# Vision tower on Trainium2: another order of loads and weight preparation at the start and at the end of the attention part

## The reference, cut to what matters

```python
# x: (32, 3, 256, 256)  ->  32 images; result (32, 257, 256)
gray  = einsum('bchw,c->bhw', x, (0.2989, 0.587, 0.114))
edges = conv3x3(gray, scharr, padding='SAME')          # two filters
edge  = abs(edges).sum(filters) / 2                    # 256 rows = 256 tokens of width 256
h = concatenate([cls_tok, edge])                       # 257 tokens
h = h + attention(layernorm(h))                        # 16 heads of 16, causal, w_qkv, w_out
h = h + ffn(layernorm(h))                              # w_gate, w_up (704x256), w_down (256x704)
# ffn: activations quantised with one scale from max|x| over ALL tokens of ALL images,
#      each weight row w: scale = max|w|/127, clip(round(w/scale))*scale
```

## Time and profile before

| | |
|---|---|
| median of 3 runs | 1169.92 us |
| the profiled execution, own time | 1166.12 us |
| its span | 1164.4 us |
| busy: PE, DVE, ACT, POOL | 949.2, 806.9, 686.8, 537.5 us |
| first scores (step 4) begin | 89.75 us |
| first instruction behind the barrier | 942.31 us |

### The profile page before, as it was taken

One profiled execution on the slowest core, in us unless ns is written; L12 is line 12 of the kernel. 1 busy time (PEld: TensorE's weight loads), 2 busy tenths in 40 slices (PEclk: granted clock), 3 DMA queues, 4 the chain that ended last, 5 costly groups with the idle time before them and its releaser, 6 DMA issues. The chain is left out here.

```text
span 1164.4 us, 28062 instructions
## 1 busy us (share of the span) xinstructions
PE 949.2 (82%) x9584; PEld 681.1 (58%) x9584; DVE 806.9 (69%) x1969; ACT 686.8 (59%) x1171; POOL 537.5 (46%) x685
## 2 busy tenths in 40 slices
PE   2268899989989999899999999989988458885665
PEld 1045666666766767676676766767666333332544
DVE  1735566777776677777767777776666359998687
ACT  0154666666666666666666666666554237785785
POOL 5243555566556555655656565556443242220000
PEclk9988999999999999999999999999998769998888
DMA  3854455555555556555455655554322005501874
GB/s 86 233 133 112 126 138 152 149 133 148 149 133 129 137 154 150 138 150 143 126 135 148 154 135 150 148 131 105 101 62 62 12 1 199 199 1 50 271 231 137
DMA packets 156101, 152.90 MB, mean 131 GB/s; under 512 B 28263, under 2 KB 152458, under 8 KB 153994
## 3 DMA queue, kind: packets, MB, share of 16 engines
q1 hardware_dynamic: 156042, 152.14, 48.2%
HBM read 67.49 MB, written 28.35 MB: 82 GB/s over the span
## 5 line engine op out<-in xcount | busy, mean ns | idle before, releaser
L542 ACT ACTIVATE prob<-ST 128x772 f32<-128x772 f32 x256 | 209.2, 817 | 149.2 <-PE ST L956 143.9
L706 DVE TENSOR_REDUCE mneg<-SX 128x2 f32<-128x258 f32 x256 | 107.5, 420 | 212.3 <-PE SX L942 211.7
L939 PE MATMUL SX<-kst,qst 96*128 96x257 bf16 (+1 forms) x1024 | 159.9, 250 | 19.1 <-DMA qst<-qpart 10.4
L708 DVE TENSOR_REDUCE mneg<-SX 128x2 f32<-128x514 f32 x256 | 174.0, 680 | 0.0
L956 PE MATMUL ST<-qst,kst 98*128 98x256 bf16 (+2 forms) x1536 | 138.7, 223 | 15.5 <-DMA qst<-mpart 15.2
L942 PE MATMUL SX<-mask_s,ident_b 128*128 128x256 bf16 x512 | 142.4, 278 | 0.0
L451 POOL TENSOR_SCALAR_AFFINE_SELECT prob<-prob 128x1016 f32<-128x1016 f32 x128 | 142.2, 1111 | 0.0
L956 PEld LDWEIGHTS ST<-qst,kst 98*128 98x128 bf16 x1536 | 120.9, 99 | 33.8 <-DMA qst<-mpart 12.7
L939 PEld LDWEIGHTS SX<-kst,qst 96*128 96x128 bf16 x1024 | 91.7, 99 | 64.3 <-issue 28.2
L975 PE MATMUL G<-prob,vaug 128*32 128x256 f32 (+2 forms) x3072 | 117.3, 282 | 14.2 <-POOL prob L451 13.2
L975 PEld LDWEIGHTS G<-prob,vaug 128*32 128x32 f32 x3072 | 83.5, 111 | 48.1 <-POOL prob L451 19.7
(11 more groups left out here) (226 smaller groups left out, 1991.8 us busy)
## 6 DMA issues: line engine op xcount, KB each, us to landing
kst<-kpart SPq DMA_DIRECT2D x192, 128.5 KB, 2.5
xin<-in_x SPq DMA_DIRECT2D x96, 256.0 KB, 4.0
gst<-gray_dram SPq DMA_DIRECT2D x96, 256.0 KB
qst<-qpart SPq DMA_DIRECT2D x192, 128.0 KB, 2.4
h_dram<-hb SPq DMA_DIRECT2D x8, 1280.0 KB, 4.6
gray_dram<-gray SPq DMA_DIRECT2D x64, 128.0 KB, 2.7
result<-oy SPq DMA_DIRECT2D x32, 256.0 KB, 3.4
hb<-h_dram SPq DMA_DIRECT2D x5, 1280.0 KB, 6.5
```

The costliest lines, as they stand in the source:

```text
L542: nc.scalar.activation(prob[:, g % 2, 2 * (u % 2):2 * (u % 2) + 2, 0:QEND], ST[:, :, 0:QEND], ACT.Exp).then_inc(exp_done, 1)
L706: nc.vector.tensor_reduce(mneg[:, 0, u // 4, 0, at], SX[:, :, S0:S0 + P + 1], AX.X, ALU.max, negate=True)
L708: nc.vector.tensor_reduce(mneg[:, 1, u // 4, 0, at], SX[:, :, S1:S1 + T], AX.X, ALU.max, negate=True).then_inc(max_done, 1)
L939: mm(SX[:, r, at:at + k], qst[par][0:SR, 2 * u + r, P * t:P * t + P], kst[par][0:SR, 2 * u + r, 0:k], start=t == 1, stop=False)
```

## The change

1. **Loads.** `load_x(0, 0)` is SP's first issue. Then come the tables, `w_qkv`, two bias rows, `w_out`, the border zeros (six transfers), and `load_x(1, 1)` of step 0. The taps (six transfers instead of twelve), the class token and `bqk` are issued by ACT at its start. One semaphore `s_const` becomes `s_tab`, `s_taps`, `s_qkv`, `s_bias`, and each user waits for its own. `w_gate` is loaded in SP's step 1, `w_up` at its end, `sel`, `wop` and `vaug` at the end of step 2.
2. **Fills.** POOL makes seven fills first; those of `vaug` and `kst` come after the gray image of steps 0 and 1.
3. **Gray buffers.** `gray_dram` is two buffers, used by even and odd images; the store waits for the read of the image before last.
4. **Gate and up weights.** DVE scales `w_gate` and rounds three tiles within the class token's chain, three in step 2, and `w_up` in step 3. PE turns `w_gate` in step 3 ahead of `values`, `w_up` at its end.
5. **Down weights.** `w_down` and the clips are loaded at the end of SP's step 32, into `xin[0]`; DVE, PE and ACT prepare them at the end of step 36, `sd_row` is copied at the end of step 37.

```diff
-    gray_dram = nc.dram_tensor("gray_dram", [IMG + 2, IMG + 2], fp32, kind="Internal").ap()
+    gray_dram = [nc.dram_tensor(f"gray_dram{i}", [IMG + 2, IMG + 2], fp32, kind="Internal").ap() for i in range(2)]
...
+                xin[0][:, :, :, :].rearrange("p c t w -> p (c t w)")[:, 0:KC * I].rearrange("p (k i) -> p k i", k=KC)]
+        sdiag = xin[1][:, 0, 0, :].rearrange("p (k q) -> p k q", k=KC)
...
+        N_BIAS, N_LATE, N_FIRST, N_INIT = 9, 11, 4, 7 + 2 * (2 + KT - 1)
+        NW0, NW2 = 3, B + LAST - 2
...
             load_x(0, 0)
+            sp.dma_start(early, table[:, C_MS:C_END]).then_inc(s_tab, 16)
+            sp.dma_start(tab[:, :], table[:, 0:P]).then_inc(s_tab, 16)
...
+            sp.wait_ge(s_init, 1)
...
+            def load_late():
+                sp.wait_ge(s_init, N_INIT)
...
+            def load_down():
+                sp.wait_ge(gray_step, 2 * (B - 1))
+                sp.dma_start(wraw[2][:, :, :], w_down.rearrange("(k p) i -> p k i", p=P)).then_inc(w_loaded[2], 16)
...
                 if valid(bW):
                     wait(sp, gray_step, bW, 2, 2)
-                    wait(sp, gst_loaded, bC, 96, 96)
+                    wait(sp, gst_loaded, bC - 1, 96, 96)
                     for t in range(QT):
-                        sp.dma_start(gray_dram[1 + P * t:1 + P * t + P, 1:1 + IMG],
+                        sp.dma_start(gray_dram[odd][1 + P * t:1 + P * t + P, 1:1 + IMG],
                                      gray[:, t, :]).then_inc(gray_saved, 16)
+                if isinstance(n, int) and n == 1:
+                    load_w(0, w_gate)
                 if valid(n + 1):
...
+                if isinstance(n, int) and n == 1:
+                    load_w(1, w_up)
+                if isinstance(n, int) and n == 2:
+                    load_late()
+                if isinstance(n, int) and n == B:
+                    load_down()
...
         @block.scalar
         def _(act):
-            act.wait_ge(s_const, 16 * N_CONST)
...
+            for dx in range(3):
+                tap = scharr[:, 0, :, dx].rearrange("(o f) y -> o f y", o=1)
+                act.dma_start(taps[GR * dx:GR * dx + GR, :, :], tap.broadcast_to([GR, 2, 3]),
+                              allow_slow_non_contiguous=True).then_inc(s_taps, 16)
...
+            act.dma_start(cls_row, cls_tok[0, :, :]).then_inc(s_bias, 16)
...
             dve.wait_ge(s_cpe, 1)
             nc.vector.tensor_copy(xT[:, :, 0], G[:, 0, 0:KC]).then_inc(s_cst, 1)
+            scales(0)
+            quantise(0, range(0, NW0))
             dve.wait_ge(s_cpe, 2)
...
+                if isinstance(n, int) and n == NW2:
+                    scales(2)
+                    quantise(2, range(KC))
+                    dve.wait_ge(gray_step, 2 * B)
+                    for k in range(KC):
+                        go(nc.vector.tensor_scalar(sdiag[:, k, :], ident, wsc[2][:, k:k + 1], None, ALU.mult))
+                    dve.wait_ge(sig_act, 1)
...
+                if isinstance(n, int) and n == B + LAST - 1:
                     dve.wait_ge(w_pe, len(TW) + 1)
-                    nc.vector.tensor_copy(sd_row[:, :], G[:, 1, 0:D]).then_inc(w_sd, 1)
+                    nc.vector.tensor_copy(sd_row[:, :], SX[:, 1, D:2 * D]).then_inc(w_sd, 1)
...
                 if ends and n == 4:
-                    pe.wait_ge(w_copied, len(TW))
-                    pe.wait_ge(w_sd, 1)
+                    pe.wait_ge(w_copied, 2 * IT)
...
+                if ends and n == 3:
+                    turn(range(0, IT))
                 values()
```

305 lines of the change are left out of this document (160 added, 145 removed).

## The result

| | before | after |
|---|---|---|
| median of 9 runs each, same chip | 1172.83 us | 1163.05 us |
| ratio, 95% interval | | 0.9921 (0.9893 to 0.9949) |
| the profiled execution, own time | 1166.12 us | 1161.52 us |
| its span | 1164.4 us | 1159.8 us |
| busy: PE, DVE, ACT, POOL | 949.2, 806.9, 686.8, 537.5 us | 954.2, 815.0, 686.2, 537.7 us |

The change makes the kernel faster, by 9.8 us of the 23.0 forecast. The forecast was 1146.9 with a range up to 1159; the median is 1163. A few runs of these kernels fell in a slower state of the chip; every ratio leaves them out, and so need not be the quotient of the two medians. Between the two profiled executions the gain is only 4.6 us of span. The execution of before that all steps were read from is a quick one: over 94 runs of that kernel beside these experiments the median was 1173 us (1165 to 1188).

The account below looks back on a forecast made before the run. Chains of latencies, in steps 0 to 3 and again at the end, were taken to bound the kernel. Opening 28.0 less 3.0 (end) and 2.0 (`load_down`) gives 23.0 us; from the median 1169.92 that is 1146.9 us, range 1139 to 1159.

Parts of the forecast that it names:

- The first scaling at 8.6, gray at 12.9: Opening, image 0: ACT scales at 8.6 us after 6.5 us of issues and the table load; gray ready at 12.9, not 36.99.
- 20.5: `w_gate` landed: Opening, DVE: `w_gate`, issued by about 14.2 us behind gray's store, lands 6.3 us later, at 20.5.
- 25.3: scales and three tiles: Opening, DVE: scales and first gate tile take 3.35 us, two more tiles 1.4, so done at 25.3.
- 27.9: the first convolution: Opening, PE: after class products of 0.7 + 1.87 us PE convolves image 0 at 27.9, not 49.19; 21.3 us earlier.
- 40.5: keys: Opening, PE: statistics and `xT` take 7.5 + 4.6 us, 0.5 for what is left; image 0's keys start 27.5 us earlier.
- 61.8: scores: End of the opening: the first scores of step 4 come at 61.8 us, not 89.75; 28.0 us earlier.
- If step 4 starts earlier, everything up to step 35 shifts by the same amount: Score steps: the work per image is as before, so the opening's 28.0 us were carried through unchanged.
- `load_down` 2.0: End of step 32, SP: issuing the down weights' load ahead of the row maxima's move costs 2.0 us, bounds 0 and 5.1.
- The end 3.0: End of the attention part: down weights on DVE delay the reciprocal's spread 2.5 us, `sd_row`'s copy adds 0.45; bounds 0.45 and 6.1.
- The second gray buffer at nothing: Gray store: costed at nothing, as the read it waits for was issued in the middle of the step before.
- B: Rival, chance 0.20: loads bound the opening, 5.5 MB at 157 GB/s before `gst` is in; PE convolves at 36, time 1155.0 us.
- D: Rival, chance 0.04: no change, 1168 us; first transfers land late anyway, or steps 4 to 6 give the head start back.

## Why the prediction was wrong, step by step

Against the profile it was made from, 23.0 us were promised in the profiled execution and 4.6 came; the 18.4 missing are 10.1 in the opening, 7.9 in the score steps up to image 24, and 0.4 from there on.

- *"The first scaling at 8.6, gray at 12.9."* 11.64 and 16.07. ACT's twelve issues took 9.5 us and not 6.5, inside the bounds of 4.3 to 12.5. The experiment that moved ScalarE's issues shows that the image lands at 9.8 anyhow: "the data isn't what ACT waits for" was wrong too. By itself it hardly mattered, as VectorE's chain was no readier for it.
- *"20.5: `w_gate` landed."* 24.16, 3.7 us of the miss. It was issued 2.8 us later than I had it, behind the store of the late gray image, and took 0.9 us longer from there.
- *"25.3: scales and three tiles."* 34.58. This is the step that failed most: 4.8 us were taken from the earlier trace rows, and it took 10.4. The prediction said of POOL's fills that "the wait behind them falls between gray images", asked only who waits for them by semaphore, and missed what they do to VectorE beside them. The change moves them from ahead of everything into the one chain that bounds the opening. 5.6 us, confirmed by moving the fills. The trace of the kernel before had the sign: the third gate tile's operations, right behind the rows that the price was read from, took 1.42 and 1.30 us instead of 0.35 and 0.29 beside POOL's two gray additions.

```profile
43.30 1.42 DVE L794 TENSOR_SCALAR h<-h,wg_inv 128x256 f32<-128x256 f32 x1
43.31 1.26 POOL L499 TENSOR_TENSOR gray<-xin 128x512 f32<-128x512 f32 x1 [6.32 <-ACT xin L620]
44.65 1.26 POOL L501 TENSOR_TENSOR gray<-gray,xin 128x512 f32<-128x512 f32 x1
44.76 1.30 DVE L796 TENSOR_SCALAR h<-h 128x256 f32<-128x256 f32 x1
```

- *"27.9: the first convolution."* 36.12, with 1.1 us less than assumed for the class products: 3.7 + 5.6 - 1.1 = 8.2.
- *"40.5: keys."* 50.27, 1.6 us more of the miss. Behind the copied `xT` the prediction left 0.5 us; it was 3.0, since PE first waits for the second image's tiles (until 48.41) and then convolves them for 1.86 us ahead of the keys. 0.9 us came back in the statistics. The lower clock level is no part of it: before, this convolution and the keys ran at it too (1.93 and 2.96 us). *"61.8: scores"*: 21.6 us on, as predicted (21.3).
- *"If step 4 starts earlier, everything up to step 35 shifts by the same amount."* This sentence holds the second half of the miss: 17.9 us at the first scores, 12.7 at image 23, 10.0 at image 24. The work per image is the same; PE's clock is not. The two falls took 2.9 and 2.7 us, and the 2.2 us up to image 0 go with 6.7 us more at the lower level; the rest, the 1.3 us between images 4 and 23 above all, stays open. The prediction treated the clock only at the very end.
- *"`load_down` 2.0."* 1.8 us from image 25 to 28, with a direct wait of 2.37 on PE. Right in size and mechanism in this profile; a second profile lost 6.0 there, and the one without the part's load still 3.0, with the clock falling at 827 and 854 us, so not all that goes there is the load's.
- *"The end 3.0."* 2.84 from image 30 to 31 and 0.41 for the copy of `sd_row`. Of the 2.84, 2.45 are there when PE spreads the reciprocals (the 2.5 of the prediction), and the projection behind it took 3.78 us against 3.39. Right, and shown by two experiments that give it back. The transposes and products of the down weights in PE's idle gap did not raise the clock for the spread (2.07 us again, as in the earlier trace rows): leaving that out of the sum was right.
- *The second gray buffer at nothing*: no run had it alone; that stays untested.
- *The rivals.* B gave 36 for the convolution, and 36.12 came, but not from B's cause: `gst` was in by then. It was `gst` alone that B described, and only once VectorE's chain was out of the way. D named steps 4 to 6 giving the head start back, through images no longer preloaded; up to image 0 they gave 2.2 and 2.7 us back and up to image 4 3.8 and 4.9, in step with the clock; with PE's waits of the opening and of the steps filled, the lead rose in them instead (26.4 at the first scores, 28.5 at image 0). Its sum needed 17 to 29.
- *What stays open.* Why both profiles of the kernel before pass steps 4 to 31 without a fall although PE waits up to 1.65 us there, and every profile of a changed kernel without matmuls in those steps has one. And why the medians differ by 9.8 us and the two profiles by 4.6: the runs that are not profiled show their mean clock, not where it fell. The feed-forward part, the same in all these kernels, takes 226.9 us from image 31's addition to the end in the kernel before, and 227.7 and 224.3 in the two profiles of the changed one, so some of it may lie there.

## What to carry to other kernels

When a change moves a fill or any other POOL operation, ask which VectorE copies, casts and `tensor_scalar` run beside it in the new place, not only who waits for its semaphore. Mark each image or tile with one operation and subtract these marks between two traces: a lead that shrinks in jumps is clock or a new wait, one that shrinks steadily is work. Don't carry a head start unchanged through a long pipeline whose PE waits a microsecond here and there, and don't price an opening by one execution: one program differed by 5 us between two profiles.

## What the runs showed of the hardware that was not expected

- Filling 2 partitions of 4112 bf16 elements took POOL 3.5 us, as long as filling 128 partitions of 4096 fp32 elements (`prob`, 3.52), and a `tensor_scalar` of 128x5 elements beside it 3.13 us instead of 0.34, while one of 64x1 took 0.15.
- PE's granted clock fell after waits of 0.7 to 2.4 us in the midst of steps in which PE is over 90% busy (in the changed kernel after 1.45 us at 177, and in its second profile after 0.75 us at 753). The Trainium skill ("TensorE: Matmul & The Clock Gate", section "HAM oscillation — how this bites in real kernels") describes waits for DMA that are longer than the bursts of matmuls between them as what lowers the clock. This case is another, as here the waits are a small share; the direction agrees: the three kernels with matmuls in those waits have PEclk 1.00 from 150 to 700 us. How rare and how uneven falls are between executions of one program (one and three in the same 95 us), only these runs show.
- The same DMA issues cost ScalarE different amounts with the moment: four of `bqk` 4.85 us at 4.8 us into the program, and 0.64 to 0.79 each when issued five microseconds later.
